# A bias row of layer 1 added by GpSimd to the residual instead of by TensorE to the product, in a two-layer graph attention kernel

## What is computed

```python
x = node_fts
mask = rel_edges == 0
for k in range(L):
    q = jnp.einsum('bnd,fd->bnf', x, Wq[k]) + bq[k]
    kk = jnp.einsum('bnd,fd->bnf', x, Wk[k]) + bk[k]
    scores = jnp.einsum('bof,bif->boi', q, kk) / SCALE
    scores = jnp.where(mask, -10000000000.0, scores)
    attn = jax.nn.softmax(scores, axis=2)
    attn = jnp.where(mask, 0.0, attn)
    ctx = jnp.einsum('boi,bid->bod', attn, x)
    ctx = jnp.einsum('bnd,ed->bne', ctx, Wc[k])
    x = layer_norm(x + ctx, ln_g[k], ln_b[k])
...
q = (x @ Wq + bq).reshape(b, n, H, HD)
...
h = h @ Wo + bo
y = h + x
```

## Time and profile before

| | before |
|---|---|
| median of 3 timed runs | 1221.51 us (1218.25 to 1221.82) |
| the profiled execution | 1220.38 us, its span 1218.7 us |
| PE busy | 1167.3 us, 96% |
| DVE busy | 985.6 us, 81% |
| ACT busy | 923.9 us, 76% |
| POOL busy | 483.1 us, 40% |
| mean granted clock of PE | 0.989 of full speed |

### The profile page before, as it was taken

The page is one execution under the profiler, slowest core; times in us unless marked ns, Lnnn a source line. Parts: engine busy times, 40 slices in busy tenths (PEclk is TensorE's granted clock), DMA queues, the critical chain, the costliest instruction groups (busy, mean ns, idle before and its releaser), DMA issues.

```text
span 1218.7 us, 28047 instructions
## 1 busy us (share of the span) xinstructions
PE 1167.3 (96%) x9452; PEld 853.8 (70%) x9452; DVE 985.6 (81%) x2680; ACT 923.9 (76%) x2112; POOL 483.1 (40%) x337
## 2 busy tenths in 40 slices
PE   5977999999999999999999999999999999999896
PEld 2854677777777777777777777777777777777563
DVE  4675788888888988888898888889888888987776
ACT  3234887888878788887878888787888878788684
POOL 1352233453363335336333533633353363334320
PEclk9799999999999999999999999999999999999999
DMA  8115152432615244261524326152432615222311
GB/s 241 36 35 143 31 166 43 122 88 60 166 37 162 48 122 88 66 160 37 162 47 122 87 64 163 36 163 46 122 88 65 162 36 155 55 70 70 104 37 36
DMA packets 170686, 114.03 MB, mean 94 GB/s; under 512 B 107185, under 2 KB 152241, under 8 KB 170545
## 3 DMA queue, kind: packets, MB, share of 16 engines
q1 hardware_dynamic: 168384, 104.37, 33.2%
q0 software_dynamic: 2160, 7.87, 1.9%
HBM read 61.87 MB, written 25.17 MB: 71 GB/s over the span
## 4 chain that ended last, share of the span: by engine, by line
PE 89%; DVE 4%; ACT 3%; issue 2%; DMA 1%; POOL 0%; DVEq 0%; ACTq 0%; SPq 0%; POOLq 0%
PE ps_j L759 36%; PE ps_t L772 22%; PE ps_j L876 9%; PE ps_s L751 8%; PE ps_s L745 7%; PE ps_j L893 4%; ACT probs L927 2%; PE ps_j L884 1%; DVE masked_s L1023 1%; PE ps_j L843 1%; DVE y_l L1173 1%; ACT pt_h L933 0%; PE ps_j L783 0%; DMA xt<-xs 0%; DMA xt<-ys 0%
## 5 line engine op out<-in xcount | busy, mean ns | idle before, releaser
L1023 DVE CUSTOM_DVE_ANT_0 masked_s<-ps_s,mask 128x512 f32<-128x512 f32 x640 | 424.3, 680 | 19.0 <-PE ps_s L751 17.1
L927 ACT ACTIVATE probs<-masked_s,nm_h 128x512 f32<-128x512 f32 x512 | 367.2, 718 | 83.1 <-DVE nm_h L1023 76.8
L772 PE MATMUL ps_t<-ident,probs 128*128 128x128 f32 x2560 | 390.8, 276 | 11.9 <-ACT pt_h L933 6.4
L772 PEld LDWEIGHTS ps_t<-ident,probs 128*128 128x128 f32 x2560 | 305.9, 142 | 96.8 <-issue 27.8
L933 ACT ACTIVATE pt_h<-ps_t 128x512 f32<-128x512 f32 x404 | 237.8, 589 | 71.2 <-PE ps_t L772 68.5
L751 PE MATMUL ps_s<-stack 128*128 128x512 f16 x512 | 194.4, 380 | 2.2 <-DVE nm_h L1023 2.1
L759 PE MATMUL ps_j<-xw,pt_l 128*128 128x256 f16 x1536 | 189.2, 274 | 0.0
L759 PEld LDWEIGHTS ps_j<-xw,pt_l 128*128 128x128 f16 x1536 | 151.3, 99 | 30.7
L600 POOL TENSOR_TENSOR rstd_L<-var_eps_L,minus_half 128x4 f32<-128x4 f32 x32 | 32.8, 1024 | 295.5 <-DVE var_eps_L L1053 295.5
L876 PE MATMUL ps_j<-pt_h,v 128*32 128x256 f32 x2048 | 125.2, 386 | 2.2 <-DVE pt_h L1030 1.9
L1058 DVE TENSOR_TENSOR pt_l<-ps_t,pt_l 128x512 f16<-128x512 f32 x128 | 88.3, 690 | 43.2 <-ACT pt_l L933 29.0
(11 more groups left out here) (116 smaller groups left out, 1609.5 us busy)
## 6 DMA issues: line engine op xcount, KB each, us to landing
stack<-bounce SPq DMA_DIRECT2D x256, 128.0 KB, 3.1
bounce<-parts SPq DMA_DIRECT2D x64, 256.0 KB, 2.7
adj_t<-adj_dram SPq DMA_DIRECT2D x30, 512.0 KB, 5.3
x<-x_dram SPq DMA_DIRECT2D x16, 512.0 KB, 3.9
out_dram<-y_f POOLq DMA_DIRECT2D x15, 512.0 KB, 3.4
stack<-adj_dram SPq DMA_DIRECT2D x2, 512.0 KB, 5.9
pt_h<-l_wc SPq DMA_DIRECT2D x2, 256.0 KB, 4.1
xt<-ys SPq DMA_TRANSPOSE x32, 4.4
```

The costliest lines, as they stand in the source:

```text
L772: last = pe.transpose(ps_t[r % 2][:, t], probs[:, r, t * P:(t + 1) * P], ident[:])
L927: act.activation(probs[:, r], masked_s[:, r], ACT.Exp, bias=nm[:, n, r:r + 1], scale=-1.0, accum_out=total[:, n, r:r + 1]).then_inc(exps, 1)
L1023: dve.tensor_tensor_reduce(out=masked_s[:, r], in0=ps_s[scores_bank(pos)][:], in1=m[:, r], scale=-scale, scalar=NONE_LEFT, op0=ALU.add, op ...
```

## The change

The row `bx1` is no longer added to the product. It is kept in fp32 (copied from PSUM once), and POOL adds it to `x1`, the residual input of layer 1, for rows that have a neighbour. Which those are is taken from the row sums of layer 0's exponentials: DVE writes min(sum, 1) into `has_l`. For each of the 16 graphs POOL multiplies the row by these flags (four tiles of 128x256) into a scratch tile (`ot` for graphs 0 and 1, `y_l` after that) and adds the scratch to `x1`; only then does `ln_done` say that x1 is ready. The 64 products of line 843, their constant matrix and PE's waits on both go.

```diff
         def _(pool):
-            pool.memset(mean_64[:], 1.0 / 64).then_inc(mean_in, 1)
...
-                pool.tensor_tensor(dst[:], dst[:], h, ALU.add).then_inc(ln_done[s], 1)
+                pool.tensor_tensor(dst[:], dst[:], h, ALU.add).then_inc(shifted if norm == 0 else ln_done[s], 1)
...
+            def add_bx(b, dst):
+
+                if early(b, 1):
+                    pool.wait_ge(bias_ready, 1)
+                    settle(pool)
+                spread = (ot[:].rearrange("p a n -> p (a n)") if early(b, 2) else y_l[:].rearrange("p t d -> p (t d)"))\
+                    .rearrange("p (t d) -> p t d", t=NT)
+                for t in range(NT):
+                    last = pool.tensor_scalar(spread[:, t], bx1[:], has_l[:, b % 2, t:t + 1], None, ALU.mult)
+                last.then_inc(bx_spread, 1)
+                pool.wait_ge(bx_spread, b + 1)
+                pool.wait_ge(shifted, b + 1)
+                pool.tensor_tensor(dst[:], dst[:], spread, ALU.add).then_inc(ln_done["L"], 1)
+
             def layer_norm_l0(b, l, dst):
                 split_y(b, l)
                 gain_and_shift("L", nth(b, l), y_l, l, dst)
+                if l == 0:
+                    add_bx(b, dst)
...
             pool.tensor_tensor(x1[:], y_f[:], shift[:, 0:1, :].to_broadcast([P, NT, D]), ALU.add)\
-                .then_inc(ln_done["L"], 1)
+                .then_inc(shifted, 1)
+            add_bx(1, x1)
...
-                    if early(b, 1) and l == 1:
-                        pe.wait_ge(bias_ready, 1)
...
-                                             lambda a, c: wc0[:, a, l, c], more=l == 1)
-                        if l == 1:
-                            last = pe.matmul(out_bank[:, t * D:(t + 1) * D], mean_64[:], bx1[:],
-                                             start=False, stop=True)
+                                             lambda a, c: wc0[:, a, l, c])
...
-                    dve.tensor_scalar(bx1[:], wide[:, 0:D], UP, None, ALU.mult).then_inc(bx1_hi, 1)
-                    dve.wait_ge(bx1_hi, 1)
-                    lower = slice(P // 2, P)
-                    dve.scalar_tensor_tensor(bx1[lower], wide[lower, 0:D], UP, bx1[lower], ALU.mult, ALU.subtract)\
-                        .then_inc(bias_ready, 1)
+                    dve.tensor_copy(bx1[:], wide[:, 0:D]).then_inc(bias_ready, 1)
...
                         dve.wait_ge(exps, NT * (blk_.slot_of("L", l, b) + 1))
+                        if l == 0:
+                            dve.tensor_scalar(has_l[:, b % 2], sum_l[:, l_buffer(b, l)], 1.0, None, ALU.min)
                         dve.tensor_scalar(some_l[:], sum_l[:, l_buffer(b, l)], SUM_FLOOR, None, ALU.max).then_inc(some_ready, 1)
```

More of the change, by code:

```diff
@@ L144, in graph_attention @@
         shift_c = sb("shift_c", [P, 2, DC])
-        bx1 = sb("bx1", [P, D], fp16)
-        mean_64 = sb("mean_64", [P, P], fp16)
+        bx1 = sb("bx1", [P, D])
         bv1 = sb("bv1", [P, D])
@@ L186, in graph_attention @@
         some_l = sb("some_l", [P, NT])
+        has_l = sb("has_l", [P, 2, NT])
         r_l = sb("r_l", [P, NT])
@@ L220, in graph_attention @@
         ident_zero, ident_in, half_in = sem("ident_zero"), sem("ident_in"), sem("half_in")
-        mean_in, bo_added, bx1_hi = sem("mean_in"), sem("bo_added"), sem("bx1_hi")
+        bo_added, shifted, bx_spread = sem("bo_added"), sem("shifted"), sem("bx_spread")
         pt_lo_ready, xw_hi = sem("pt_lo_ready"), sem("xw_hi")
@@ L913, in _ @@
             pe.wait_ge(ident_in, 1)
-            pe.wait_ge(mean_in, 1)
             program(walk)
```

## The result

| | before | after |
|---|---|---|
| median | 1219.88 us (1217.36 to 1221.82, 4 runs) | 1239.53 us (1238.04 to 1240.28, 4 runs) |
| the profiled execution | 1220.38 us, span 1218.7 | 1238.04 us, span 1236.3 |
| POOL busy | 483.1 us | 579.7 us |

A forecast was written before the change was run, and what follows sets the result against it. PE was taken to bound the loop without a gap, and the prologue to decide the sign: -6.1 - 0.6 + 4.6 + 1.7 + 1.0 = +0.6 us on 1220.9, so 1221.5 us (own range 1219.5 to 1223.5, overall 1217.7 to 1224.8).

The forecast's parts named there:

- the block's price: POOL's added work per graph: four TENSOR_SCALAR at 0.55 us plus one addition of 2.37, 4.6 us.
- The upper bound: POOL's block: its four TENSOR_SCALAR can't be dearer than two-input work of the same size, so at most 4.8 us.
- the two terms of 1.7 and 1.0 us: Prologue: 1.7 us for DVE held by POOL's addition, 1.0 us for PE's clock falling after the longer pause.
- Rival (D): Loop: POOL's moved split holds DVE's mask, PE's scores wait; +13 us, 1234 us, from a block over some 5 us; 5%.
- the cover: Loop: 14.2 us of POOL idle time against 4.6 added, so the block costs 0 there.
- Removed from PE: Line 843's 64 products gone: -6.1 us in the loop (0.44 a turn), -0.6 in the prologue.
- the whole block lands on the chain: Prologue: graph 1's block stands before the reciprocal root of graph 0's layer 1, delaying everything behind: +4.6 us.
- The hold at 59.39 (+1.7): Prologue: DVE's flag or maximum of graph 1 is held by POOL's addition until 61.55, making PE 1.7 us later.
- the clock's +1.0: Prologue: PE's pause before 63.04 grows to about 2.8 us and its clock falls, +1.0 us (bounds 0 and 1.4).
- rival (A): Prologue: DVE isn't held at 59.39 and the clock stays up; sum -2.1 or -3.3, 1218.8 (1217.6) us; 22%.
- Behind the longer pause: Prologue, PE's pause before 89.39: it comes with one clock fall anyway, so nothing was added.
- rival (C): Prologue stretches further: two clock falls in place of one, each lasting longer; another 1.4 to 3.4 us, 1223 to 1225; 11%.

The follow-up runs named there:

- e7: The kernel of e4 with four different one-input forms in place of POOL's four equal TENSOR_SCALAR, scratch only; one timed execution 1225.4 us.
- e6: The kernel of e5 with the final norm's last POOL addition cut into four of 128x256; median 1213.36 us, ratio 0.9954.
- e1: The changed kernel with the flags given as both scalars of each new POOL TENSOR_SCALAR (two operations); median 1223.22 us, ratio 1.0031.
- e3: The changed kernel with DVE's two mask jobs two tiles and one tile later in the loop's table; median 1223.22 us, ratio 1.0021.
- e2: The changed kernel without POOL's block, the row added nowhere, DVE still writing the flags; median 1216.70 us, ratio 0.9979.
- e5: The kernel of e1 with graph 1's prologue block moved between gain and shift of graph 0's layer-1 norm; median 1215.82 us, ratio 0.9979.
- e9: The kernel before with only the final norm's last POOL addition cut into four of 128x256; median 1219.92 us, ratio 1.0002.
- e8: The kernel before with eight one-input TENSOR_SCALAR and eight copies added on POOL behind each turn's split, scratch only; one timed execution 1219.29 us.
- e4: The kernel before, all products kept, with POOL's block (scratch only) and DVE's flags added; median 1237.91 us, ratio 1.0148.

## Why the prediction was wrong

**The step that failed is the block's price.** "I take line 665, the same operation and shape": line 665 has two operations in one instruction, the new one has one, and that form takes 0.92 us. The upper bound, two-input work of the same size, was taken as if no one-input form could be dearer; e7 has one at 0.93, where the two-input pieces of e6 cost 0.70 (2.78 / 4). What the turns lost hangs on it: 6.05 us in place of 4.6. With the block at its forecast price (e1) the kernel took 1223.2 us, inside the forecast's own range, though partly by luck: the two terms of 1.7 and 1.0 us didn't come, and in their place 3 us of the saving in the turns and 2.7 us of the last stages were missing. Rival (D) was priced from "a block longer than some 5 us" with a hold of 1.5 us, of which 1.0 would be felt, 13 us in sum on top of the forecast. Measured were 6.05 and 1.4, and the whole of the 1.4 was felt: the turns grew by 11.0 where the forecast had -6.1, so what stands beside the 13 is 17.1. (D) had the mechanism and was 5 us short of the time. It had 5% because of a bound that was no bound.

**In the loop**, the cover was right for POOL's queue and wrong for DVE. The 14.2 us of idle time took the block without harm (e3), while the moved split was, by my own reckoning, still running for 0.2 us when the mask began. A margin that small should have carried far more than 5%.

**Removed from PE**: 0.44 us a turn is right (e6: 70.63). But in e1, e2 and e5 only 0.3 came out, since DVE's hold before the layer-1 residual became the next thing late. I had read this hold in the earlier trace rows and used it for the prologue alone. Two halves of one mechanism: e9 without the saving and e5 without the cut each lack what e6 has.

**In the prologue**, "the whole block lands on the chain" is right, at 6.06 us. **The hold at 59.39 (+1.7) didn't come.** In the kernel after DVE met POOL's one-input operations, which don't hold it, and was done before the addition began:

```profile
57.09 3.64 POOL L657 TENSOR_SCALAR ot<-bx,has_l 128x256 f32<-128x256 f32 x4 [1.50 <-DVE bx L1120]
...
58.86 0.16 DVE L1166 TENSOR_SCALAR has_l<-sum_l 128x4 f32<-128x4 f32 x1
58.92 0.17 DVE L1167 TENSOR_SCALAR some_l<-sum_l 128x4 f32<-128x4 f32 x1
...
62.41 1.46 PE L775 MATMUL ps_j<-xt,wq 128*128 128x512 f16 x6 [1.06 <-DVE y_l L1181]
```

PE's pause stayed at 1.06 us, so **the clock's +1.0** fell away too. Both stood at the lower bound I had given, 0. In e1, with the block as I had priced it, DVE's maximum started at 59.19 us just as POOL's addition did, and took 0.16 us: the margin of 0.2 us that rival (A) named, decided its way.

**Behind the longer pause** I had added nothing for the clock. For the twelve products after it that held: they take 2.72 us, the half rate of the earlier trace rows, behind 8.81 us, 7.30 us and 2.96 us of waiting alike (the three rows of e5's section). Beyond them it held in the kernel after (granted clock 0.59 from 94 to 99 us, then 1.00 to 110), but not in e1: 0.50 from 93 to 99 us, with PE busy for 5.73 of the 6, and another fall from 105 to 110 (0.66), where the kernel before has 1.00 in both. That is what rival (C) described, in a kernel whose pause was the shorter one; its price isn't separated. The same prologue differs by itself: the first copy of x2 starts at 103.53 us in the kernel before and at 100.93 in e8, whose edit comes only later. The windows of e8 over two stretches in which the kernel before had a granted clock of 0.58 and 0.81:

```profile
50.00:60.00 10.00, 10.00 (x63) 8.85 (x64) 4.94 (x19) 0.60 (x1) 4.99 (x3) 0.69 0.44 107
86.00:95.00 9.00, 6.61 (x39) 3.93 (x39) 6.63 (x16) 3.76 (x10) 5.50 (x4) 1.00 0.31 58
```

So the 4.8 us that the prologue seems to give is 7.4 against that start (my sum with 6.05 for the block and without the two terms that fell away is 5.5), and single profiles can't settle the last 2 us of such sums. The same goes for the 2 to 3 us that the last stages of the kernel after and of e1 took more. The traces show one thing that goes with them. Where the stages behind the last turn take 88.6 to 89.5 us (the kernel after, e1, e4, e7), the granted clock is 0.83 in the second 10 us of them. Where they take 86.3 to 87.2 (the kernel before, e3, e5, e6, e9), it is 0.83 in the first 10 us; in e2 (87.1) and e8 (87.4) it is 1.00 in both. That the place of the fall costs the time is not shown.

## What to carry to other kernels

Take a duration only from a row with the same number of operations as well as the same shape and inputs, and treat an upper bound as one only if a row of the same form stands behind it. Moving work on POOL moves each two-input operation behind it against DVE: list where those meet DVE's SBUF-to-SBUF operations, and if one stands within half a microsecond of such a meeting, give it a real chance, move the small job in the table, or cut the POOL operation in pieces. When the bound engine gets faster by a little, look for what had been late by just less than that.

## What the hardware showed that I had not expected

- POOL's TENSOR_SCALAR on 128x256 fp32 takes 0.92 us with one operation and 0.55 with two (e1, e7), so multiplying twice by a flag of 0 or 1 is the cheaper way to multiply once.
- One-input work of POOL hardly holds DVE (0.25 us at most in 26 masks of e8), while a two-input operation of 128x1024 held a 128x4 operation for up to 1.9 us, and one of 128x256 for 0.4 (e6).
- A gap on PE costs more than the idle time printed in front of it. Three gaps of 0.82 us in sum lengthened the distances of starts by 1.31 us, since the idle time begins at the end of the product before (0.27 or 0.38 us after its start), while an unhindered product starts 0.11 or 0.22 us after the one before.
